# The state-space input of a fused token block read modes first and twice over, its on-chip turn dropped, and the text copy issued later

## The chip, the cores and the metric

The kernel runs on one core of a Trainium2 chip. The metric is device time in microseconds (us) of one execution. The engines that matter here are TensorE (PE), VectorE (DVE), ScalarE (ACT), GpSimd (POOL) and SyncE (SP), which issues most DMAs; each runs its own instruction stream, and semaphores join them.

## What is computed

A batch of 32 sequences is built from a diagonal state-space convolution kernel (128 rows of length 1024 for each) and 77 rows of text; one attention layer and one linear layer with low-rank parts follow. Only the first part is touched by the change:

```python
dt = exp(log_dt)                                  # (128, 2)
dt_Lambda = dt[:, None, 0] * Lambda[None, :, 0] + 1j * (dt[:, None, 1] * Lambda[None, :, 1])
Wc = (x[..., 0] + 1j * x[..., 1]) * num * _reciprocal(den * Lam, 1e-07)   # x: (32, 128, 64, 2)
K = einsum('chn,hnl->chl', Wc, exp(dt_Lambda[..., None] * pos - P_max[..., None])).real
h = concatenate([K, txt], axis=1)                 # (32, 128 + 77, 1024)
h = h + attention(layernorm(h));  h = h + linear(layernorm(h))
```

`x` holds for each of 32 sequences c, 128 rows h and 64 modes n a real and an imaginary weight.

## The kernel before

The program is a row of blocks with a barrier between them: `ssm` (the state-space part and the text copy), `prep_qkv` (weights of the projections), `attention`, `prep_out`, `output`. The order inside a block is written by hand, engine by engine, in the functions under `@block.sync`, `@block.gpsimd`, `@block.scalar`, `@block.vector` and `@block.tensor`. No scheduler moves anything: each engine takes its instructions in the order of the text and stops at its `wait_ge` lines.

`ssm` has a first part that builds tables and a loop of 16 chunks of 8 rows. In the loop (L210 to L214 on POOL, L375 to L388 on DVE, L405 to L417 on PE, L259 to L273 on ACT, L174 to L179 on SP) POOL makes the products `u` and `u2` from the weights `wr`, `wi` and the place factors `gg`; DVE makes the steps `es` from the tables `tab` and `ab` and adds `u2` to `u`; PE multiplies; ACT copies PSUM to `ob`; SP stores `ob` to the scratch tensor `hcat`. `ob` has two halves, so the copies of chunk 2 (L263, L264) wait for the stores of chunk 0.

The weights must lie with modes on the partitions, real on one half and imaginary on the other as the sums need it: `wr` and `wi` are each [128, 32 sequences, 128 rows], where partitions 64 to 127 hold the same as 0 to 63. The kernel before makes this layout on the chip. SP loads `x` into `x_sb` (the memory of `ob`) with the 128 rows h on the partitions (L168). ACT copies the real parts twice side by side into `twice[0]` (in the memory of `stage`, L231), POOL copies the imaginary parts into `twice[1]` (in the memory of `wr`, L201). PE turns them by 64 transposes against `ident` (L403), and ACT empties their PSUM tiles `pt` by 16 copies (L242, in `inputs`) into `wi` and then `wr`, eight after the second sine and eight after the fourth.

Around this lie the tables. DVE makes `f`, the two bases (L302), the small arguments, and four fractions (L323, L324) from what ACT has shifted into `turned` (L228, the memory of `es`). ACT then takes exponentials (L233, L235) and sines (L244, L246, and the four L249). POOL makes the arguments of the sizes (L197) and multiplies two of the sine tables by the sizes (L205). DVE has a long chain of small operations (L327 to L368) whose result is `gg`; it begins with a wait for the sine of L244 (L326), and its end releases the first product of POOL (L206, L213) and leads to DVE's own L373. The text copy, one DMA of 9856 KB from `txt` to `hcat`, is issued by ACT as its second instruction (L221). SP issues the load of the query weights into `stage` (L173) once the tables and the transposes are done.

Of the kernel before, what the change touches and what calls it, by code (L numbers as in the profile page):

```python
# [7 lines left out]
F32 = mybir.dt.float32  # L8
# [3 lines left out]
ALU = mybir.AluOpType  # L12
# [4 lines left out]
P = 128  # L17
B = 32
H = 128
N = 64  # L20
# [3 lines left out]
S = H + TXT  # L24
# [9 lines left out]
LA, LB, LR = 4, L // 4, 16  # L34
# [36 lines left out]
def ssm(nc, x, txt, log_dt, lam, hcat, ahead, peak):  # L71
# [4 lines left out]
    with ExitStack() as ctx:  # L76
        sb = lambda n, s, d=F32: ctx.enter_context(nc.sbuf_tensor(n, s, d))
        sem = lambda n: ctx.enter_context(nc.semaphore(n))
        wr = sb("wr", [P, B, H])
        wi = sb("wi", [P, B, H])  # L80
        ident = sb("ident1", [P, P])
        lam_sb = sb("lam_sb", [P, 2])
        ldt = sb("ldt", [P, H, 2])
        dt = sb("dt", [P, H, 2])
# [4 lines left out]
        a = sb("a", [P, H])  # L89
        b = sb("b", [P, H])  # L90
        f = sb("f", [P, H])
# [21 lines left out]
        u = sb("u", [P, 2, HC, LA, B])  # L113
        u2 = sb("u2", [P, 2, HC, LA, B])


        x_sb = ob[:].rearrange("p k j l -> p (k j l)").rearrange("p (c n t) -> p c n t", n=N, t=2)
        turned = es[:].rearrange("p k m j l -> p (k m j l)").rearrange("p (t h r) -> p t h r", t=4, r=LR)
        base = u[:].rearrange("p k j l c -> p (k j l c)").rearrange("p (h r) -> p h r", r=LR)
        base2 = u2[:].rearrange("p k j l c -> p (k j l c)").rearrange("p (h r) -> p h r", r=LR)  # L120
        bases = (base, base2)
        size = ahead[0].rearrange("p k n -> p (k n)")[:, 0:2 * H * LR].rearrange("p (k h r) -> p k h r", k=2, r=LR)
        twice = (ahead[0].rearrange("p k n -> p (k n)")[:, 2 * H * LR:].rearrange("p (c m) -> p c m", m=P), wr)
        ps = [ctx.enter_context(nc.psum_tensor(f"ps1_{i}", [P, 2, LB], F32)) for i in range(4)]
        pt = [ctx.enter_context(nc.psum_tensor(f"pt1_{i}", [P, 4, P], F32)) for i in range(2)]
        ab = [ctx.enter_context(nc.psum_tensor(f"ab1_{i}", [P, 2, HC, LR], F32)) for i in range(2)]

        in_small, in_x, txt_in = sem("in_small"), sem("in_x"), sem("txt_in")
        pool_c, dve_c = sem("pool_c"), sem("dve_c")
        dt_ok, waves_ok, la_sin_ok, la_exp_ok = sem("dt_ok"), sem("waves_ok"), sem("la_sin_ok"), sem("la_exp_ok")  # L130
        ab_ok, base_ok, turned_ok, frac_ok, sine_ok = (sem("ab_ok"), sem("base_ok"), sem("turned_ok"),
                                                       sem("frac_ok"), sem("sine_ok"))
        size_arg, size_ok, tab_cd, tab_ab = sem("size_arg"), sem("size_ok"), sem("tab_cd"), sem("tab_ab")
        args_ok, la_ok = sem("args_ok"), sem("la_ok")
        iota_ok, ident_ok = sem("iota_ok"), sem("ident_ok")
        xt_filled, xt_read = sem("xt_filled"), sem("xt_read")
        twice_ok = [sem("twice_ok0"), sem("twice_ok1")]
        gg_ok, u12_ok, ab_in, e_ok = sem("gg_ok"), sem("u12_ok"), sem("ab_in"), sem("e_ok")
        u_ok, mm_done, k_read = sem("u_ok"), sem("mm_done"), sem("k_read")
        stored = [sem("stored0"), sem("stored1")]  # L140
# [22 lines left out]
        @block.sync  # L163
        def _(sp):
            sp.dma_start(lam_sb[0:N, :], lam).then_inc(in_small, 16)
            sp.dma_start(lam_sb[N:P, :], lam).then_inc(in_small, 16)
            sp.dma_start(ldt[:], log_dt.rearrange("(o h) t -> o h t", o=1).broadcast_to([P, H, 2])).then_inc(in_small, 16)
            sp.dma_start(x_sb.rearrange("p c n t -> p c (n t)"), x.rearrange("c h n t -> h c (n t)")).then_inc(in_x, 16)  # L168

            sp.wait_ge(tab_ab, 2)  # L170
            sp.wait_ge(tab_cd, 2)
            sp.wait_ge(xt_filled, 2 * B // 4)
            sp.dma_start(ahead[0], ahead[1]).then_inc(ahead[2], 16)  # L173
            for ch in range(NCH):  # L174

                sp.wait_ge(k_read, (ch + 1) * HC // 2)
                for la in range(LA):
                    sp.dma_start(hview[la, :, ch * HC:(ch + 1) * HC, :],
                                 ob[la * B:(la + 1) * B, ch % 2, :, :]).then_inc(stored[ch % 2], 16)  # L179
            for q in range(2):  # L180
                sp.wait_ge(stored[q], 16 * LA * NCH // 2)

        @block.gpsimd
        def _(pool):
            chain = Chain(pool, pool_c)
            pool.iota(ila[:], pattern=[[LB, LA]], base=0, channel_multiplier=0,
                      allow_small_or_imprecise_dtypes=True).then_inc(iota_ok, 1)
            pool.iota(iqr[:, 0, :], pattern=[[LR, LR]], base=0, channel_multiplier=0,
                      allow_small_or_imprecise_dtypes=True).then_inc(iota_ok, 1)
            pool.iota(iqr[:, 1, :], pattern=[[1, LR]], base=0, channel_multiplier=0,  # L190
                      allow_small_or_imprecise_dtypes=True).then_inc(iota_ok, 1)
            chain(pool.memset(ident[:], 0.0))
            pool.affine_select(out=ident[:], in_=ident[:], compare_op=ALU.not_equal, fill=1.0, base=0,
                               pattern=[[-1, P]], channel_multiplier=1).then_inc(ident_ok, 1)
            pool.wait_ge(ab_ok, 1)
            for k in range(2):
                pool.tensor_tensor(size[:, k], per_row(a[:]), per_step(iqr[:, k, :]), ALU.mult).then_inc(size_arg, 1)  # L197

            pool.wait_ge(in_x, 16)
            for k in range(2):  # L200
                pool.tensor_copy(twice[1][:, :, k * N:(k + 1) * N], x_sb[:, :, :, 1]).then_inc(twice_ok[1], 1)  # L201
            pool.wait_ge(size_ok, 1)
            for t in range(2):
                pool.wait_ge(sine_ok, t + 1)
                pool.tensor_tensor(tab[:, t], tab[:, t], size[:, 0], ALU.mult).then_inc(tab_ab, 1)  # L205
            pool.wait_ge(gg_ok, 1)  # L206
            pool.wait_ge(xt_read, 2 * B // 4)

            pool.wait_ge(frac_ok, 4)
            for ch in range(NCH):  # L210
                if ch >= 2:
                    pool.wait_ge(mm_done, (ch - 1) * HC // 2)
                pool.tensor_tensor(u[:, ch % 2], by_mode(wr, ch), by_place(0, ch), ALU.mult).then_inc(u12_ok, 1)  # L213
                pool.tensor_tensor(u2[:, ch % 2], by_mode(wi, ch), by_place(1, ch), ALU.mult).then_inc(u12_ok, 1)  # L214

        @block.scalar
        def _(act):
            act.wait_ge(in_small, 48)
            act.activation(dt[:], ldt[:], ACT.Exp).then_inc(dt_ok, 1)

            act.dma_start(hcat.rearrange("(c s) d -> c s d", s=S)[:, H:S, :], txt).then_inc(txt_in, 16)  # L221

            act.wait_ge(args_ok, 1)
            act.activation(ex[:], args[:, 0].rearrange("p k h -> p (k h)"), ACT.Exp).then_inc(waves_ok, 1)
            act.activation(th[:], args[:, 0].rearrange("p k h -> p (k h)"), ACT.Tanh, scale=0.5).then_inc(waves_ok, 1)
            for t in range(4):
                act.wait_ge(base_ok, t // 2 + 1)
                act.activation(turned[:, t], bases[t // 2], ACT.Identity, bias=phase[:, t:t + 1]).then_inc(turned_ok, 1)  # L228
            act.wait_ge(in_x, 16)
            for k in range(2):  # L230
                act.copy(twice[0][:, :, k * N:(k + 1) * N], x_sb[:, :, :, 0]).then_inc(twice_ok[0], 1)  # L231
            act.wait_ge(la_ok, 1)
            act.activation(ela[:], fla[:, 0], ACT.Exp).then_inc(la_exp_ok, 1)  # L233
            act.wait_ge(size_arg, 2)
            act.activation(size, size, ACT.Exp).then_inc(size_ok, 1)  # L235

            def inputs(ns):
                for n in ns:
                    act.wait_ge(xt_filled, n + 1)
                    c = 4 * (n % (B // 4))  # L240
                    dst = (wi if n < B // 4 else wr)[:, c:c + 4, :]
                    act.copy(dst, pt[n % 2][:]).then_inc(xt_read, 1)  # L242

            act.activation(trig[:], turns[:], ACT.Sin, scale=TWO_PI).then_inc(waves_ok, 1)  # L244
            act.wait_ge(la_ok, 2)
# [1 line left out]
            for t in range(4):  # L247
                act.wait_ge(frac_ok, t + 1)
                act.activation(tab[:, t], turned[:, t], ACT.Sin, scale=TWO_PI).then_inc(sine_ok, 1)  # L249
                if t % 2:  # L250
                    inputs(range(4 * (t - 1), 4 * (t + 1)))

            def factors(ch):

# [4 lines left out]
            def results(ch):  # L259
                for j in range(HC // 2):  # L260
# [3 lines left out]
                        act.wait_ge(stored[ch % 2], 16 * LA * (ch // 2))  # L264
                    act.copy(ob[:, ch % 2, 2 * j:2 * j + 2, :], ps[n % 4][:]).then_inc(k_read, 1)

            act.wait_ge(tab_ab, 2)
            factors(0)
            factors(1)
# [123 lines left out]

        @block.tensor
        def _(pe):
            pe.wait_ge(ident_ok, 1)
            for t, n0 in ((1, 0), (0, B // 4)):
                pe.wait_ge(twice_ok[t], 2)
                for n in range(n0, n0 + B // 4):
                    if n >= 2:  # L400
                        pe.wait_ge(xt_read, n - 1)
                    for k in range(4):
                        m = pe.transpose(pt[n % 2][:, k, :], twice[t][:, 4 * (n - n0) + k, :], ident[:])  # L403
                    m.then_inc(xt_filled, 1)
            for ch in range(NCH):  # L405
                pe.wait_ge(u_ok, ch + 1)
                pe.wait_ge(e_ok, ch + 1)
                for j in range(HC):
                    n = (ch * HC + j) // 2
                    if j % 2 == 0 and n >= 4:  # L410
                        pe.wait_ge(k_read, n - 3)
                    last = 0 if j < SUMMED else 1
                    for k in range(last + 1):
                        m = pe.matmul(ps[n % 4][:, j % 2, :], u[:, ch % 2, j].rearrange("p a c -> p (a c)"),
                                      es[:, ch % 2, k, j, :], start=k == 0, stop=k == last)
                    if j % 2:
                        m.then_inc(mm_done, 1)  # L417
# [1060 lines left out]
```

## Time and profile before

| | us |
|---|---|
| three runs of the kernel before | 3353.92, 3346.96, 3353.59 (median 3353.59) |
| the profiled execution, its time | 3349.05 |
| its span from first to last instruction | 3347.3 |
| the block `ssm` in it, until the loads of the next block are issued | 212.0 |
| PE busy, share of the span | 91% |
| DVE, ACT, POOL busy | 60%, 33%, 31% |

In a row of the order of time the first number is the start in us from the start of the span, the second the length of the piece (of all `xN` instructions in it together), then engine, line, operation, output and inputs by the program's names; `[15.16 <-ACT trig L244]` says that the engine sat idle for 15.16 us before it, and what ended that. SPq and ACTq are the queues that issue DMAs; such a row is the issue, not the transfer.

### The profile page before, as it was taken

The page shows a single profiled execution, that of the slowest core. Times are in us where ns is not written, and L with a number is a line of the kernel's source. Part 1 is how long each engine was busy: PE and PEld are TensorE (multiplying, and loading weights), DVE is VectorE, ACT ScalarE, POOL GpSimd, SP SyncE. Part 2 cuts the span into 40 slices and gives each one's busy share as a digit, 9 for nine tenths or more (in the row PEclk, how much of TensorE's full clock was granted, in tenths as well). Part 3 has the DMA queues.
Part 4 walks back from the last instruction along what each step waited for, and adds up shares of the span by engine and source line. Part 5 has one row for each costly group of instructions (what it writes and reads, how often), then busy time and mean ns, then how long its engine had stood idle before and what let it go on. Part 6 is the DMA issues. An engine that isn't in the chain of part 4 may idle for free. (4 is left out here: it accounts for less than half of the span.)

```text
span 3347.3 us, 82139 instructions
## 1 busy us (share of the span) xinstructions
PE 3030.5 (91%) x29056; PEld 2239.5 (67%) x29056; DVE 2001.2 (60%) x4714; ACT 1111.7 (33%) x2452; POOL 1025.4 (31%) x1400
## 2 busy tenths in 40 slices
PE   1848799999999999999999997799999999999999
PEld 1637688888898888888888984244545454544444
DVE  7975576767676767676776765444444444443443
ACT  4331345454455455454545454210101010100100
POOL 3730344444444444444444454011101110110110
PEclk9978899999999999999999995599999999999999
DMA  4643222222222222222222213111221122122111
GB/s 147 169 126 106 47 79 56 80 53 80 56 80 55 79 68 65 70 63 78 55 78 56 71 48 136 38 67 59 75 75 64 68 75 75 56 75 75 69 62 46
DMA packets 235388, 249.64 MB, mean 75 GB/s; under 512 B 169753, under 2 KB 196505, under 8 KB 234785
## 3 DMA queue, kind: packets, MB, share of 16 engines
q1 hardware_dynamic: 234768, 234.69, 23.7%
q10 hardware_dynamic: 240, 10.09, 0.9%
q8 instruction: 214, 3.51, 0.4%
q14 instruction: 166, 1.35, 0.1%
HBM read 114.26 MB, written 80.61 MB: 58 GB/s over the span
## 5 line engine op out<-in xcount | busy, mean ns | idle before, releaser
L732 POOL TENSOR_SCALAR_AFFINE_SELECT p<-p 128x256 f32<-128x256 f32 (+1 forms) x768 | 335.3, 437 | 921.4 <-ACT p L760 899.5
L842 DVE TENSOR_REDUCE mx<-psS 77x2 f32<-77x410 f32 (+1 forms) x768 | 449.3, 613 | 242.5 <-PE psS L944 155.5
L962 PE MATMUL psJ<-xth,qh 128*128 128x205 f16 x2048 | 529.5, 259 | 10.6 <-DVE qsl L850 8.0
L964 PE MATMUL psJ<-xth,ql 128*128 128x205 f16 x2048 | 525.4, 257 | 0.0
L963 PE MATMUL psJ<-xtl,qh 128*128 128x205 f16 x2048 | 523.9, 256 | 0.0
L760 ACT ACTIVATE p<-psT,escale 128x410 f32<-128x410 f32 (+1 forms) x768 | 411.3, 572 | 282.0 <-PE psT L906 206.3
L738 POOL TENSOR_TENSOR pl<-p,ph 128x410 f16<-128x410 f32 (+1 forms) x512 | 447.1, 893 | 105.2 <-ACT ph L767 97.3
L1295 POOL TENSOR_TENSOR hb<-h,bias_sb 128x1024 f32<-128x1024 f32 x52 | 122.1, 2349 | 1045.3 <-DVE h L1337 1045.3
L929 PE MATMUL psO<-vh,pl 128*128 128x33 f16 (+2 forms) x3072 | 347.4, 187 | 0.0
L929 PE MATMUL psO<-vh,ph 128*128 128x33 f16 (+2 forms) x3072 | 341.6, 188 | 5.1 <-POOL pl L738 3.7
L929 PE MATMUL psO<-vl,ph 128*128 128x33 f16 (+2 forms) x3072 | 343.8, 187 | 0.0
L767 ACT CAST ph<-p 128x410 f16<-128x410 f32 (+1 forms) x768 | 334.1, 500 | 5.7 <-POOL p L732 5.6
L1337 DVE SCALAR_TENSOR_TENSOR h<-ps5O,osc,h_in 128x512 f32<-128x512 f32 x104 | 78.1, 751 | 429.0 <-PE ps5O L1384 429.0
L929 PEld LDWEIGHTS psO<-vh,ph 128*128 128x128 f16 (+2 forms) x3072 | 324.5, 116 | 6.8 <-issue 6.4
L929 PEld LDWEIGHTS psO<-vh,pl 128*128 128x128 f16 (+2 forms) x3072 | 325.6, 115 | 0.0
L929 PEld LDWEIGHTS psO<-vl,ph 128*128 128x128 f16 (+2 forms) x3072 | 323.9, 113 | 0.3
L1382 PE MATMUL ps5O<-woh,ath 128*128 128x512 f16 x832 | 317.1, 381 | 1.4 <-DVE atl L1322 1.4
L1383 PE MATMUL ps5O<-wol,ath 128*128 128x512 f16 x832 | 316.8, 381 | 0.0
L1382 PE MATMUL ps5F<-wfh,xth 128*128 128x512 f16 x832 | 315.3, 379 | 1.6 <-DVE xtl L1322 1.6
L1384 PE MATMUL ps5O<-woh,atl 128*128 128x512 f16 x832 | 316.6, 381 | 0.0
L1383 PE MATMUL ps5F<-wfl,xth 128*128 128x512 f16 x832 | 315.3, 379 | 0.0
L1384 PE MATMUL ps5F<-wfh,xtl 128*128 128x512 f16 x832 | 315.3, 379 | 0.0
(241 smaller groups left out, 6080.8 us busy)
## 6 DMA issues: line engine op xcount, KB each, us to landing
a_in<-acat SPq DMA_DIRECT2D x52, 512.0 KB, 4.8
h_in<-hcat SPq DMA_DIRECT2D x52, 512.0 KB, 4.2
qst<-qsh SPq DMA_DIRECT2D x512, 51.2 KB, 2.1
out<-y SPq DMA_DIRECT2D x51, 512.0 KB, 3.0
hcat<-ob SPq DMA_DIRECT2D x64, 256.0 KB, 3.7
xin<-hcat SPq DMA_DIRECT2D x32, 512.0 KB
acat<-ao SPq DMA_DIRECT2D x32, 512.0 KB
qst<-qsl SPq DMA_DIRECT2D x256, 51.2 KB, 2.1
```

The source lines that it names most:

```text
L732: pool.affine_select(out=v, in_=v, compare_op=ALU.is_ge, fill=0.0, base=0, pattern=[[0, v.shape[1]], [1, w]], channel_multiplier=-1).then_ ...
L738: pool.tensor_tensor(view(pl, g % 2, k), view(p32, g % 2, k), view(ph, g % 2, k), ALU.subtract).then_inc(lo_pool, 1)
L760: act.activation(view(p32, g % 2, k), ps_view(psT[(g + k) % 2], k), ACT.Exp, scale=(escale[:, 0:1] if k < 2 else escale[0:TXT, 0:1])).then ...
L767: act.copy(view(ph, g % 2, k), view(p32, g % 2, k)).then_inc(hi_done, 1)
L842: dve.tensor_reduce(dst, v, AX.X, ALU.max).then_inc(s_read, 1)
L929: m = pe.matmul(o[0:T[t], t, r, :], p, v[0:T[j], j, g, :], start=n == 0, stop=n == len(list_) - 1)
L962: pe.matmul(ps[:, 0:S], wh[:, k, c], xth[:, par, k, :], start=k == 0, stop=False)
L963: pe.matmul(ps[:, 0:S], wh[:, k, c], xtl[:, par, k, :], start=False, stop=False)
L964: m = pe.matmul(ps[:, 0:S], wl[:, k, c], xth[:, par, k, :], start=False, stop=k == KC - 1)
L1382: pe.matmul(ps[h][:], th[:, k, :], wh[:, k, c], start=k == 0, stop=False)
L1383: pe.matmul(ps[h][:], th[:, k, :], wl[:, k, c], start=False, stop=False)
L1384: m = pe.matmul(ps[h][:], tl[:, k, :], wh[:, k, c], start=False, stop=k == KC - 1)
```

## The change

The host hands the kernel `x` as [2, 128, 32, 128]: real or imaginary, then the 64 modes twice, then sequence and row. Two DMAs bring the two halves straight into `wr` and `wi`. What turned the input on the chip is gone: `ident`, the four copies into `twice`, the 64 transposes, the PSUM tiles `pt` and the 16 copies out of them, and the semaphores between them. The wait of POOL before its first product and of ACT before the text copy is now for both input DMAs. The text copy stands behind the fourth sine. Everything behind `ssm` is as it was.

```diff
@@ tiles and semaphores
-        ident = sb("ident1", [P, P])
-        x_sb = ob[:].rearrange("p k j l -> p (k j l)").rearrange("p (c n t) -> p c n t", n=N, t=2)
-        twice = (ahead[0].rearrange("p k n -> p (k n)")[:, 2 * H * LR:].rearrange("p (c m) -> p c m", m=P), wr)
-        pt = [ctx.enter_context(nc.psum_tensor(f"pt1_{i}", [P, 4, P], F32)) for i in range(2)]
@@ SP
-            sp.dma_start(x_sb.rearrange("p c n t -> p c (n t)"), x.rearrange("c h n t -> h c (n t)")).then_inc(in_x, 16)
+            sp.dma_start(wr[:], x[0]).then_inc(in_x, 16)
+            sp.dma_start(wi[:], x[1]).then_inc(in_x, 16)
 
             sp.wait_ge(tab_ab, 2)
             sp.wait_ge(tab_cd, 2)
-            sp.wait_ge(xt_filled, 2 * B // 4)
             sp.dma_start(ahead[0], ahead[1]).then_inc(ahead[2], 16)
@@ POOL
-            chain(pool.memset(ident[:], 0.0))
-            pool.affine_select(out=ident[:], in_=ident[:], compare_op=ALU.not_equal, fill=1.0, base=0,
-                               pattern=[[-1, P]], channel_multiplier=1).then_inc(ident_ok, 1)
-            pool.wait_ge(in_x, 16)
-            for k in range(2):
-                pool.tensor_copy(twice[1][:, :, k * N:(k + 1) * N], x_sb[:, :, :, 1]).then_inc(twice_ok[1], 1)
-            pool.wait_ge(xt_read, 2 * B // 4)
+            pool.wait_ge(in_x, 32)
@@ ACT
-            act.dma_start(hcat.rearrange("(c s) d -> c s d", s=S)[:, H:S, :], txt).then_inc(txt_in, 16)
-            act.wait_ge(in_x, 16)
-            for k in range(2):
-                act.copy(twice[0][:, :, k * N:(k + 1) * N], x_sb[:, :, :, 0]).then_inc(twice_ok[0], 1)
-            def inputs(ns):
-                for n in ns:
-                    act.wait_ge(xt_filled, n + 1)
-                    c = 4 * (n % (B // 4))
-                    dst = (wi if n < B // 4 else wr)[:, c:c + 4, :]
-                    act.copy(dst, pt[n % 2][:]).then_inc(xt_read, 1)
-                if t % 2:
-                    inputs(range(4 * (t - 1), 4 * (t + 1)))
+            act.wait_ge(in_x, 32)
+            act.dma_start(hcat.rearrange("(c s) d -> c s d", s=S)[:, H:S, :], txt).then_inc(txt_in, 16)
             act.wait_ge(tab_ab, 2)
@@ PE
-            for t, n0 in ((1, 0), (0, B // 4)):
-                pe.wait_ge(twice_ok[t], 2)
-                for n in range(n0, n0 + B // 4):
-                    if n >= 2:
-                        pe.wait_ge(xt_read, n - 1)
-                    for k in range(4):
-                        m = pe.transpose(pt[n % 2][:, k, :], twice[t][:, 4 * (n - n0) + k, :], ident[:])
-                    m.then_inc(xt_filled, 1)
@@ kernel
+        if name == "x":
+            a = np.concatenate([a.transpose(3, 2, 0, 1)] * 2, axis=1)
```

The order of ACT from its shifts to its first factors, before (the last row is the first of eight such PSUM copies; the other two sines and eight more copies follow):

```order
6 L228 ACTIVATE es<-u,phase 128x2048 [waits base_ok] x4
7 L231 COPY stage<-ob 128x32x64 [waits in_x]
8 L231 COPY stage<-ob 128x32x64
9 L233 ACTIVATE ela<-fla 128x512 [waits la_ok]
10 L235 ACTIVATE stage<-stage 128x4096 [waits size_arg]
11 L244 ACT_TABLE_LOAD
12 L244 ACTIVATE trig<-turns 128x768
13 L246 ACTIVATE tla<-wla 128x1024 [waits la_ok]
14 L249 ACTIVATE tab<-es 128x2048 [waits frac_ok] x2
15 L242 COPY wi<-pt_0 128x512 [waits xt_filled]
```

The same place of ACT in the changed kernel (its line numbers are lower: L216 is the exponential of the sizes, L223 the four sines, L240 the text copy, L229 the factors):

```order
5 L212 ACTIVATE es<-u,phase 128x2048 [waits base_ok] x4
6 L214 ACTIVATE ela<-fla 128x512 [waits la_ok]
7 L216 ACTIVATE stage<-stage 128x4096 [waits size_arg]
8 L218 ACT_TABLE_LOAD
9 L218 ACTIVATE trig<-turns 128x768
10 L220 ACTIVATE tla<-wla 128x1024 [waits la_ok]
11 L223 ACTIVATE tab<-es 128x2048 [waits frac_ok] x4
12 L240 DMA hcat<-in_txt 32x7x11264 [waits in_x]
13 L229 COPY ab_0<-tab 128x256 [waits tab_ab]
14 L229 COPY ab_1<-tab 128x256
```

No wait for the input stands ahead of the exponentials and sines any more; the first one is that of the text copy.

The order of POOL from the size arguments to the first chunk, before:

```order
12 L197 TENSOR_TENSOR stage<-a,iqr 128x2048 [waits ab_ok]
13 L197 TENSOR_TENSOR stage<-a,iqr 128x2048
14 L201 COPY wr<-ob 128x32x64 [waits in_x]
15 L201 COPY wr<-ob 128x32x64
16 L205 TENSOR_TENSOR tab<-tab,stage 128x2048 [waits sine_ok,size_ok]
17 L205 TENSOR_TENSOR tab<-tab,stage 128x2048 [waits sine_ok]
18 L213 TENSOR_TENSOR u<-wr,gg 128x1024 [waits frac_ok,xt_read,gg_ok]
```

The same place of POOL in the changed kernel:

```order
10 L186 TENSOR_TENSOR stage<-a,iqr 128x2048 [waits ab_ok]
11 L186 TENSOR_TENSOR stage<-a,iqr 128x2048
12 L191 TENSOR_TENSOR tab<-tab,stage 128x2048 [waits sine_ok,size_ok]
13 L191 TENSOR_TENSOR tab<-tab,stage 128x2048 [waits sine_ok]
14 L199 TENSOR_TENSOR u<-wr,gg 128x1024 [waits frac_ok,in_x,gg_ok]
```

The wait for the input has moved from ahead of the table products to the first product of the loop.

## Rows read from the trace of the kernel before

**Rows 1.** ACT in order of time, from the shifts to the first factors
```profile
20.21 7.67 ACT L228 ACTIVATE es<-u,phase 128x2048 f32<-128x2048 f32 x4
44.64 3.97 ACT L231 COPY stage<-ob 128x2048 f32<-128x2048 f32 x2 [16.77 <-DMA ob<-in_x]
48.52 0.63 ACT L233 ACTIVATE ela<-fla 128x512 f32<-128x512 f32 x1
...
55.66 3.69 ACT L249 ACTIVATE tab<-es 128x2048 f32<-128x2048 f32 x2
...
59.26 1.05 ACT L242 COPY wi<-pt 128x512 f32<-128x512 f32 x2
...
75.75 0.69 ACT L257 COPY ab<-tab 128x256 f32<-128x256 f32 x2
```

**Rows 2.** DVE in order of time, from its last fraction to the loop
```profile
37.39 2.29 DVE L324 TENSOR_TENSOR es<-es,tab 128x2048 f32<-128x2048 f32 x1
54.84 0.42 DVE L327 SCALAR_TENSOR_TENSOR t<-ex,th 128x256 f32<-128x256 f32 x1 [15.16 <-ACT trig L244]
...
57.41 0.35 DVE L336 SCALAR_TENSOR_TENSOR cc<-em,lam_sb,cc 128x128 f32<-128x128 f32 x1
57.68 4.69 DVE L337 SCALAR_TENSOR_TENSOR cc<-em,lam_sb,cc 128x128 f32<-128x128 f32 x1
62.40 4.51 DVE L338 TENSOR_TENSOR cc<-cc 128x128 f32<-128x128 f32 x1
66.83 0.28 DVE L339 TENSOR_TENSOR cc<-cc 128x128 f32<-128x128 f32 x1
...
77.44 0.42 DVE L368 TENSOR_SCALAR gg<-fla 64x512 f32<-64x512 f32 x1
77.89 6.83 DVE L373 TENSOR_TENSOR tab<-tab,stage 128x2048 f32<-128x2048 f32 x2
...
103.43 4.48 DVE L382 TENSOR_TENSOR es<-tab,ab 128x2048 f32<-128x2048 f32 x2 [3.56 <-ACT ab L257]
```

**Rows 3.** POOL in order of time, first part of the block
```profile
44.67 4.00 POOL L201 COPY wr<-ob 128x2048 f32<-128x2048 f32 x2 [30.58 <-DMA ob<-in_x]
57.70 9.06 POOL L205 TENSOR_TENSOR tab<-tab,stage 128x2048 f32<-128x2048 f32 x2 [9.03 <-ACT tab L249]
77.94 4.63 POOL L213 TENSOR_TENSOR u<-wr,gg 128x1024 f32<-128x1024 f32 x1 [11.18 <-DVE gg L368]
```

**Rows 4.** PE and ACT in order of time, at the loop's start
```profile
93.67 14.87 PE L414 MATMUL ps<-es,u 128*128 128x256 f32 x56 [18.43 <-DVE u L388]
...
111.00 0.59 ACT L265 COPY ob<-ps 128x512 f32<-128x512 f32 x1 [1.56 <-PE ps L414]
...
116.18 0.59 ACT L265 COPY ob<-ps 128x512 f32<-128x512 f32 x1 [1.14 <-PE ps L414]
```

**Rows 5.** Stretches: length, busy (instructions) by engine, PE clock, DMA share, GB/s
```profile
60.00:62.00 2.00, 2.00 (x10) 1.78 (x11) 2.00 (x1) 1.01 (x3) 2.00 (x1) 1.00 0.00 0
70.00:72.00 2.00, 2.00 (x10) 1.77 (x11) 1.92 (x5) 1.02 (x3) 0.00 (x0) 0.50 0.00 0
86.00:98.00 12.00, 4.33 (x10) 3.53 (x11) 11.96 (x6) 0.58 (x1) 6.53 (x3) 0.50 0.86 346
99.00:100.00 1.00, 1.00 (x7) 0.87 (x6) 0.87 (x1) 0.59 (x1) 0.00 (x0) 1.00 0.00 0
130.00:160.00 30.00, 27.91 (x124) 23.33 (x125) 27.23 (x17) 11.77 (x23) 23.76 (x10) 1.00 0.61 150
```

**Rows 6.** DMA queue of the text copy and DMA issues, 0 to 110 us
```profile
q10 hardware_dynamic: 240, 10.09, 27.2%
...
hcat<-in_txt ACTq DMA_DIRECT2D x1, 9856.0 KB, 39.5
stage<-in_L_attn_wq SPq DMA_DIRECT2D x1, 4096.0 KB, 12.7
...
ob<-in_x SPq DMA_DIRECT2D x1, 0.5 KB, 41.7
```

More of the change, by code:

```diff
@@ L122, in ssm @@
         size = ahead[0].rearrange("p k n -> p (k n)")[:, 0:2 * H * LR].rearrange("p (k h r) -> p k h r", k=2, r=LR)
-        twice = (ahead[0].rearrange("p k n -> p (k n)")[:, 2 * H * LR:].rearrange("p (c m) -> p c m", m=P), wr)
         ps = [ctx.enter_context(nc.psum_tensor(f"ps1_{i}", [P, 2, LB], F32)) for i in range(4)]
-        pt = [ctx.enter_context(nc.psum_tensor(f"pt1_{i}", [P, 4, P], F32)) for i in range(2)]
         ab = [ctx.enter_context(nc.psum_tensor(f"ab1_{i}", [P, 2, HC, LR], F32)) for i in range(2)]
         in_small, in_x, txt_in = sem("in_small"), sem("in_x"), sem("txt_in")
-        pool_c, dve_c = sem("pool_c"), sem("dve_c")
+        dve_c = sem("dve_c")
         dt_ok, waves_ok, la_sin_ok, la_exp_ok = sem("dt_ok"), sem("waves_ok"), sem("la_sin_ok"), sem("la_exp_ok")
@@ L134, in ssm @@
         args_ok, la_ok = sem("args_ok"), sem("la_ok")
-        iota_ok, ident_ok = sem("iota_ok"), sem("ident_ok")
-        xt_filled, xt_read = sem("xt_filled"), sem("xt_read")
-        twice_ok = [sem("twice_ok0"), sem("twice_ok1")]
+        iota_ok = sem("iota_ok")
         gg_ok, u12_ok, ab_in, e_ok = sem("gg_ok"), sem("u12_ok"), sem("ab_in"), sem("e_ok")
@@ L184, in _ @@
         def _(pool):
-            chain = Chain(pool, pool_c)
             pool.iota(ila[:], pattern=[[LB, LA]], base=0, channel_multiplier=0,
@@ L395, in _ @@
         def _(pe):
-            pe.wait_ge(ident_ok, 1)
-            for t, n0 in ((1, 0), (0, B // 4)):
-                pe.wait_ge(twice_ok[t], 2)
-                for n in range(n0, n0 + B // 4):
-                    if n >= 2:
-                        pe.wait_ge(xt_read, n - 1)
-                    for k in range(4):
-                        m = pe.transpose(pt[n % 2][:, k, :], twice[t][:, 4 * (n - n0) + k, :], ident[:])
-                    m.then_inc(xt_filled, 1)
             for ch in range(NCH):
@@ L1464 @@
     for name in _INS:
-        a = np.ascontiguousarray(inputs[name])
+        a = np.asarray(inputs[name])
+        if name == "x":
+            a = np.concatenate([a.transpose(3, 2, 0, 1)] * 2, axis=1)
+        a = np.ascontiguousarray(a)
         if a.dtype == np.bool_:
```

## The prediction

> **What bounds the kernel now.** I read the order of time of ACT first, since the change takes a wait out of it; then DVE, which ACT releases; POOL, which both feed; then the stretches and the DMAs. The input lands late: 41.7 us after its issue, beside a text copy that takes 39.5 us [rows 6]. ACT has finished its shifts at 20.21 + 7.67 = 27.88, sits idle for 16.77 us until the input is there, and copies it before it goes on to the exponential of L233 at 48.52 [rows 1]. So ACT does everything from L233 on 48.52 - 27.88 = 20.64 us later than its own work would let it. POOL has nothing to do in that time (30.58 us idle) [rows 3]. What reaches the end is smaller, and stands in DVE: it finishes its fourth fraction at 37.39 + 2.29 = 39.68 and waits 15.16 us for the sine of L244 [rows 2]. From 54.84 on, it runs without a gap to `gg` at 77.86, releases POOL's first product at 77.94 [rows 2, 3], and PE starts the loop at 93.67 [rows 4]. In the loop DVE is busy for 27.23 of 30 us [rows 5], so it sets the pace, and the block's end moves by what its start moves. The 15.16 us are therefore about what can be had; ACT's 20.64 are not, because DVE's own fractions end only at 39.68.
>
> **The change, part by part.**
>
> *The wait and the copies on ACT go (L231).* ACT starts L233 at 27.88 (its argument was ready before, at DVE's pace). From L233 to the first sine L249 it took 55.66 - 48.52 = 7.14 us [rows 1], the table load among it; so the first sine starts at 35.02. Trig is then ready well before DVE asks for it at 39.68. The first three sines ask for their fractions at 35.0, 36.9 and 38.7; DVE begins the second step of the fourth at 37.39 [rows 2], so the third is there in time, and the two before it, each two DVE operations earlier, as well.
>
> *A new meeting of POOL and DVE.* POOL's two products L205 take 9.06 us together and began 2.04 us after the first sine started [rows 1, 3]; now they begin at 37.1, in DVE's last fraction. While POOL ran them before, two tiny DVE operations took 4.69 and 4.51 us, where their neighbours of the same shape took 0.35 and 0.28 [rows 2]. So one of the two engines stands while the other works: 4.34 + 4.23 = 8.57 us of DVE's chain were such standing. DVE's chain from L327 to `gg` without it is 77.86 - 54.84 - 8.57 = 14.45 us. Whatever the order in which they take turns, DVE has its fraction and its chain to do and stands for POOL's whole 9.06 us: `gg` comes at 39.68 + 14.45 + 9.06 = 63.19 instead of 77.86. That is 14.67 us earlier. In other words: the idle 15.16, less 9.06 - 8.57 = 0.49 of more standing. The bounds: if DVE didn't have to stand at all, `gg` would come at 54.13, a gain of 23.7; I take the sum with standing, since two rows show it with exactly this POOL instruction. The other side is that DVE stands twice, once for the last fraction and then again for a later pair, but there is no later POOL instruction before `gg`.
>
> The Trainium skill, "SBUF — State Buffer", section "Who interferes with whom", says the same of VectorE operations with two inputs in SBUF beside a GpSimd one that reads it: whoever is first holds the shared ports for a whole instruction. Without it the sum would be the 23.7; the trace agrees with it by the two rows above.
>
> *The fourth sine* waits for a fraction that POOL's first product may push to 39.68 + 4.53 = 44.2; it ends at about 46.1 and is wanted by DVE's L373 at 63.2. Hidden by 17 us.
>
> *The transposes and PSUM copies go.* 64 transposes on PE, 16 copies of about 0.53 to 0.59 us on ACT between the sines [rows 1]: they ended at about 75.9, ahead of `gg` at 77.86, so they weren't what POOL waited for. Nothing is gained by itself. But at 63.2 they would be late, so the gain needs their removal. The factors (L257 at 75.75 before) wait for POOL's second product, now at about 48.7 to 49, and are wanted only at about 63.2 + 6.8 = 70: hidden. The identity and POOL's two copies are early or in idle time: nothing.
>
> *The input as two DMAs of 2 MB.* It is first wanted by POOL at 63.2, and at about 46 by ACT ahead of the text copy. The trace doesn't show this load. The nearest row is the load of query weights, as large (4096 KB) and alone on the queues: 12.7 us [rows 6]; the farthest is the present input, 2 MB in 41.7 us beside the text. Issued at about 3, both halves land at about 16 by the first and at 3 + 2 x 41.7 = 86 by the second. I take the first: nothing runs beside them now. In that case 47 us of slack are left.
>
> *The text copy moves behind the fourth sine* and is issued at about 47. Its issue costs ACT 0.7 us, hidden since ACT then waits for POOL until 48.7. Its packets were 27.2% of 110 us on the DMA engines, that is 29.9 us of their time [rows 6]; at most it takes the 39.5 us of the row. So it ends between 78 and 87. SP issues the query weights when L373 is done, at 84.7 - 14.7 = 70, so these two now overlap, and behind the weights on the same queue stand the stores of chunk 0, issued from 103.1 - 14.7 = 88.5. The weights had 0.86 of 12 us [rows 5], 10.3 us of DMA time. Text done by 78 or so: text and weights end at 70 + 1.5 + 6.5 + 10.3 = 88, just ahead of the stores, and nobody waits. At the bound of 39.5: about 98; the stores of chunk 0 are 1 MB, and the loop's 150 GB/s at a DMA share of 0.61 over 30 us [rows 5] make 18.3 / 4.5 = 4.1 us a MB, so they land at 102, and ACT's first copy of chunk 2, before at 111.00, now at 96.3, would stand 5.7 us. It can catch up (116.18 - 111.00) - 3 x 0.59 = 3.4 us, because it is paced by PE at 1.73 us a copy and needs 0.59 [rows 4]. So between 0 and 2.3 us; I take 0, since 29.9 is the packets' own time and 39.5 has the old input in it.
>
> *PE's clock.* The matmuls of chunk 0 run at a granted clock of 0.50, the lower level of 1.2 GHz, until about 99, when the clock rises to the full 2.4 GHz [rows 5]. They started at 93.67 after 18.43 us of idleness [rows 4]. In the changed kernel PE does nothing before 79, so I take the same slow start: no change. The clock column says 1.00 at 60 to 62, after a far longer pause; but ten transposes take the same 2 us there as at 70 to 72 with 0.50 [rows 5], so the column cannot be believed before its first change.
>
> The Trainium skill, "TensorE: Matmul & The Clock Gate", section "What's actually happening", has the throttled clock as the state from which activity releases the engine; the trace agrees by the equal pace of the transposes. If the column were right the start would be fast instead, which is the second rival.
>
> *The sum:* -15.16 + 0.49 = -14.7 us. On the profiled execution: 3349.05 - 14.7 = 3334.4. The median of the three runs lies 4.5 us above that execution; on it: 3353.59 - 14.7 = 3338.9, which is my time.
>
> **The rivals.**
>
> 1. DVE doesn't stand for POOL in the new place, because its last fraction and the early part of its chain slip past. For it: only L337 and L338 are seen standing. Against: both inputs of nearly every operation of the chain are of the same sort. Gain up to 23.7: 3329.9.
>
> 2. The clock is full in chunk 0. Then PE doesn't hold DVE at chunk 2, where DVE was idle for 3.56 us [rows 2]; chunk 0's matmuls would take about 6.3 us instead of 8.9, gain 2.6 more: 3336.3. Against: the equal pace of the transposes.
>
> 3. Text copy, query weights and stores pile up as worked out above: 2.3 us given back, 3341.2.
>
> 4. The change does what it says in `ssm`, and the rest of the program takes it back. Everything behind the block's barrier starts earlier by the same amount, with the same instructions, so I see no mechanism; but the runs alone are spread over 7 us. Within 0.2%: about 3350.
>
> 5. Slower than before: the new loads are slow. If 4 MB come at the rate of the old input, they land at 86, POOL's first product moves from 77.94 to 86, and the time is 3353.59 + 8.1 = 3361.7. It decides at a landing of 77.9: earlier is a gain, later a loss. Against it: the old input had the text copy beside it and rows of 512 bytes, and the new rows are 16 KB each.
>
> **How the numbers follow.** The forecast 0.64, rival 1 0.06, rival 2 0.08, rival 3 0.08, rival 4 0.09, rival 5 0.05. A measurement of this kernel can tell about 0.2% (6.7 us) from no change. Faster by more than that: the first four, 0.86; within it 0.09; slower 0.05. The range reaches down to the lowest run less the gain with rival 2 (3346.96 - 17.3 = 3329.7), a little beyond it for rival 1, and up to the edge of "no change" (3346.9): 3328 to 3347.
>
> **What would show it.** ACT's exponential of L233 (now L214) at about 27.9; the wait of DVE for trig gone; two DVE operations of some 4.5 us or a stretched fraction between 37 and 49; `gg` at 63.2; the first matmul at 79.0 at the lower clock; the input landed by 20; the text copy landed between 78 and 87; the loads of the next block issued at 197.3 instead of 212.0. It would be wrong if the input landed after 63, if DVE's chain took another length than 14.5 plus 9.1, or if ACT stood at the first copy of chunk 2.

## The result, and the profile after

The changed kernel takes 3369.5 us (median, 3336.9 to 3379.0), the kernel before 3349.5 us beside it (3345.6 to 3365.4). The ratio of the means is 1.0044, with a 95% interval of 1.0024 to 1.0063: slower by 0.44%, where 0.44% faster was forecast (the medians alone make 1.0060: four of the twenty executions of the changed kernel took under 3355 us, the others 3362 to 3379). The profiled execution took 3362.45 us with a span of 3360.6, 13.3 more than before.

In `ssm` it went as forecast. ACT, DVE, POOL and SP in order of time, after (start, length, engine, line, then the idle time before it; they answer to [rows 1 to 4]):

```profile
29.35 0.61 ACT L214 ACTIVATE ela<-fla 128x512 f32<-128x512 f32 x1
...
45.47 1.91 ACT L223 ACTIVATE tab<-es 128x2048 f32<-128x2048 f32 x1 [3.50 <-DVE es L298]
45.48 0.72 ACTq L240 DMA_DIRECT2D hcat<-in_txt  x1
...
97.18 0.58 ACT L237 COPY ob<-ps 128x512 f32<-128x512 f32 x1 [1.56 <-PE ps L379]
```

```profile
6.91 0.15 DVE L260 TENSOR_SCALAR g<-lam_sb 128x1 f32<-128x1 f32 x1 [5.30 <-DMA ldt<-in_L_tok_log_dt]
...
38.95 6.48 DVE L298 TENSOR_TENSOR es<-es,tab 128x2048 f32<-128x2048 f32 x1
45.36 4.72 DVE L301 SCALAR_TENSOR_TENSOR t<-ex,th 128x256 f32<-128x256 f32 x1
...
63.69 0.42 DVE L342 TENSOR_SCALAR gg<-fla 64x512 f32<-64x512 f32 x1
```

```profile
38.52 11.28 POOL L191 TENSOR_TENSOR tab<-tab,stage 128x2048 f32<-128x2048 f32 x2 [22.86 <-ACT tab L223]
64.20 4.63 POOL L199 TENSOR_TENSOR u<-wr,gg 128x1024 f32<-128x1024 f32 x1 [14.40 <-DVE gg L342]
```

```profile
79.93 14.80 PE L379 MATMUL ps<-es,u 128*128 128x256 f32 x56 [79.93 <-DVE u L362]
...
198.19 0.41 SPq L414 DMA_DIRECT2D st_k<-in_L_attn_wk  x1
```

The last row is the first load of the next block, which the kernel before issued at 211.99: 13.8 us won. The DMA issues of the first 110 us (KB, then us to landing), after:

```profile
hcat<-in_txt ACTq DMA_DIRECT2D x1, 9856.0 KB, 36.3
stage<-in_L_attn_wq SPq DMA_DIRECT2D x1, 4096.0 KB, 21.5
...
wr<-in_x SPq DMA_DIRECT2D x1, 2048.0 KB, 9.4
wi<-in_x SPq DMA_DIRECT2D x1, 2048.0 KB, 13.8
ldt<-in_L_tok_log_dt SPq DMA_DIRECT2D x1, 128.0 KB, 4.7
```

The loss lies behind it. `output` starts its first product later, before (L1382) and after (L1347):

```profile
2164.91 0.61 PE L1382 MATMUL ps5O<-woh,ath 128*128 128x512 f16 x1 [1.40 <-DVE atl L1322]
```

```profile
2178.26 0.61 PE L1347 MATMUL ps5O<-woh,ath 128*128 128x512 f16 x1 [1.40 <-DVE atl L1287]
```

That is 13.35 us late, the whole difference of the spans, so `output` itself is unchanged. What lies between, whose code the change does not touch, takes 27.2 us more: 13.8 won at its start, 13.35 lost at its end. Nearly all of it is in `attention`, whose first product comes 13.8 us earlier than before (244.27 and 258.07) and whose last ends 13.8 us later (2077.1 and 2063.3). `attention` is mostly a hardware loop of 13 turns of two steps; the jump back to its start is called the wrap here. A turn took 109.66 us before and 111.39 after (the mean of the 11 turns between the 12 wraps), which makes 19.0 of the 27.2 us; the rest is lost in the steps before the first wrap and behind the last. The views of waits over 460 to 2140 us (us in total, times, longest) say who waits longer; before, then after:

```profile
ACT vsh L775 <- DMA vl<-vsl: 81.5, 16, 6.2
...
PE psT L906 <- ACT p L760: 13.0, 19, 1.5
```

```profile
ACT vsh L740 <- DMA vl<-vsl: 88.9, 14, 7.1
...
PE psT L868 <- issue: 38.7, 12, 3.5
...
PE psT L871 <- ACT p L725: 26.5, 23, 2.4
```

TensorE's wait for ACT's exponential `p` doubles; its wait for "issue" (for nothing that the view names) at L868 is 37.8 us before (L903) and 38.7 after, 12 times some 3 us, at the wrap. One turn shows the chain, before and after (SP's row, ACT, PE in order of time):

```profile
1187.43 2.96 SPq L635 DMA_DIRECT2D kst<-ksh  x4
...
1204.35 0.37 ACT L775 CAST vsh<-psJ 128x256 f16<-128x256 f32 x1 [4.52 <-DMA vl<-vsl]
```

```profile
1179.79 2.43 SPq L600 DMA_DIRECT2D kst<-ksh  x4
1182.27 3.33 SPq L600 DMA_DIRECT2D kst<-ksl  x4
...
1188.17 5.77 SPq L600 DMA_DIRECT2D qst<-qsh  x8
1193.99 2.68 SPq L600 DMA_DIRECT2D qst<-qsl  x4
...
1198.75 0.59 SPq L628 DMA_DIRECT2D vl<-vsl  x1
```

```profile
1203.61 0.37 ACT L740 CAST vsh<-psJ 128x256 f16<-128x256 f32 x1 [6.41 <-DMA vl<-vsl]
...
1204.54 0.48 PE L871 MATMUL psT<-qst,kst 98*77 98x308 f16 x1 [1.73 <-ACT p L725]
```

SP issues a row of 24 small copies (`restack`), some 0.6 us each, then the copy of `vl`. ACT may not write `vsh` before these copies have read it; behind that wait stands the exponential, and TensorE waits for this. Four issues take 2.43 us, but 3.33 in the second group of this row (before, the one group with a fetch takes 2.96). In that group's time one packet was fetched on the queue q8 (DMA queues, 1182.2 to 1185.6, and the whole execution before and after). q8 brings TensorE's own program; it is read so because each of TensorE's waits at the wrap has such a packet at its start (see e8):

```profile
q8 instruction: 1, 0.02, 2.4%
```

```profile
q8 instruction: 214, 3.51, 0.5%
```

```profile
q8 instruction: 225, 3.69, 0.5%
```

3.51 MB in 214 packets is 16.4 KB a packet; by the period of 256 instructions that e9 and e10 find, that is 64 bytes an instruction. Of the issues of L635 between 470 and 1840 us that took over 0.9 us, 87 of 91 had such a fetch beginning within 0.5 us of their start, of the shorter ones 53 of 1111; after, 90 of 91 and 84 of 1086. So a long issue nearly always has a fetch beside it, but many a fetch has no long issue. The critical row, the one ahead of the second step of a turn, meets one fetch in 10 of 12 turns before (from its first issue to its last it takes 15.3 us on average) and two in every turn after (16.2 us). The whole execution has 11 fetches more than before, about one a turn. After the wait the clock falls, and TensorE goes at the lower of its two levels, 1.2 GHz, for some 3 us (length, busy by engine, granted clock in the third number from the end; the first stretch lies ahead of the wait, the second behind it):

```profile
1199.00:1200.00 1.00, 1.00 (x11) 0.90 (x10) 0.82 (x6) 0.00 (x0) 0.00 (x0) 1.00 0.88 327
1204.60:1207.20 2.60, 2.60 (x16) 2.30 (x17) 1.67 (x3) 2.10 (x5) 1.82 (x4) 0.50 0.08 30
```

So the suspicion was: the change made TensorE's compiled program 130 instructions shorter (64 transposes are 64 weight loads and 64 matmuls, and 2 waits), which moves `attention` by half a block of 256 against the borders at which the program is fetched. "Place" below means where TensorE's program stands against these borders.

### The profile page after: what moved, and what is told of

Read it like the earlier page. It is cut to its first block and busy times, and to the rows that moved or that the text cites. A ratio compares the mean times of both kernels' runs of the same rounds, so it can differ in the third digit from the quotient of the medians.

```text
span 3360.6 us, 81794 instructions
## 1 busy us (share of the span) xinstructions
PE 3013.5 (90%) x28800; PEld 2235.7 (67%) x28992; DVE 2001.5 (60%) x4714; ACT 1098.8 (33%) x2434; POOL 1021.9 (30%) x1396
## 5 line engine op out<-in xcount | busy, mean ns | idle before, releaser
L1347 PE MATMUL ps5O<-woh,ath 128*128 128x512 f16 x832 | 317.1, 381 | 1.4 <-DVE atl L1287 1.4
L1347 PE MATMUL ps5F<-wfh,xth 128*128 128x512 f16 x832 | 315.3, 379 | 1.6 <-DVE xtl L1287 1.6
```

Of the source, the lines that this page charges most:

```text
L1347: pe.matmul(ps[h][:], th[:, k, :], wh[:, k, c], start=k == 0, stop=False)
```

## Experiments

The ratios are to runs of the kernel before on the same chip (medians 3354.8 us beside e1 to e4, 3348.2 beside e5 to e8, 3349.2 beside e9 to e12). All kernels but e5 and e12 compute everything. "Fillers" are instructions that do nothing, put ahead of TensorE's first wait in `ssm`, where it has nothing to do until about 80 us:

```diff
+        fill = sem("fill")
@@ ssm, first lines of @block.tensor
+            for _ in range(130):
+                pe.sem_inc(fill, 1)
```

T1 is the theory of the place of TensorE's program; the rivals are named in the expectations. Where an expectation puts TensorE's wait in front of the row scores, it follows my first reading; the view of waits puts it one instruction earlier, at `psT` for ACT.

**e1, changed kernel with 130 fillers (the old place).** 

> The changed kernel with 130 semaphore increments as fillers at the start of TensorE's part of the state-space block, where TensorE is idle for 79 us. They take the place of the 130 instructions (64 weight loads, 64 matmuls, 2 waits) that the change took out of TensorE's program, so that everything behind stands where it stood before in that program. Theory T1 (the place of TensorE's program against its 16 KB fetches decides when a fetch meets SyncE's row of small DMA issues in the attention loop, and that costs the loop its 27 us): the block keeps its gain of 13.8 us, the attention loop runs as in the kernel before, and the time is about 14 us below the kernel before: 3335, ratio 0.996. Rival T2 (the loop is slower because it starts 14 us earlier, or because the larger input has moved the tensors in memory): no help, the time stays about 3369, ratio 1.005.

Measured: 3341.6 us (3335.3 to 3346.0), ratio 0.9958 [0.9943, 0.9974]. One fetch in the row in 11 of 12 turns, 15.3 us, a turn 109.98 us. TensorE's wait for ACT:

```profile
PE psT L874 <- ACT p L728: 17.6, 21, 2.1
```

**e2, kernel before with 126 fillers (the place of the changed one).** 

> The kernel before with 126 semaphore increments at the start of TensorE's part of the state-space block: 126 + 130 = 256 instructions of 64 bytes are one fetch of 16 KB, so TensorE's program stands against the fetches as in the changed kernel, with nothing else changed. T1: the attention loop becomes 20 to 27 us slower, 3369 to 3377, ratio about 1.007, with the same wait of TensorE at the row scores of the loop's second half. T2: unchanged within 0.2%, ratio 1.000.

Measured: 3377.0 us (3375.1 to 3388.7), ratio 1.0073 [1.0054, 1.0092]. Two fetches in the row, 16.2 us, a turn 111.96.

```profile
PE psT L909 <- ACT p L763: 26.6, 22, 3.0
```

The loss is larger than the time shows: in the profiled execution the input landed in 37.5 us instead of 41.7, and `ssm` was done at 207.38 instead of 211.99, so what lies between `ssm` and `output` takes 31.6 us more than before.

These two are the crossed test: the loss goes with the place of TensorE's program, not with the new input or the earlier start. e1 has all of the change and is faster than before; e2 has none of it and is slower. The other engines' programs, also a little shorter, weren't put back in e1 and aren't needed for it: the packets on q14, the other queue of kind "instruction", fell from 177 before to 118 after, and are 118 in e1 too and 179 in e2.

**e3 and e4, 64 and 194 fillers.** 

> The changed kernel with 64 fillers: half way between the changed kernel's place and the old one. T1: a time of its own between 3330 and 3375; the wait of TensorE at the row scores in the loop's second half follows how many of its fetches fall into SyncE's issues ahead of it. I expect about 3350. T2: 3369, as with any number of fillers.

> The changed kernel with 194 fillers, 64 beyond the old place. T1: a time of its own between 3330 and 3375, not equal to that with 130 fillers; I expect about 3345. T2: 3369, as with any number of fillers.

Measured: e3 3363.9 us, 1.0025 [1.0000, 1.0049]; e4 3346.5 us, 0.9974 [0.9963, 0.9985]. e3 was expected near 3350 and came out 14 us higher; e4 met its 3345. Both have two fetches in every row (16.3 and 16.2 us), but in e4 TensorE waits little for ACT:

```profile
PE psT L874 <- ACT p L728: 11.4, 15, 2.2
PE psT L871 <- DMA qst<-ml: 10.4, 15, 1.0
```

So the number of fetches in one row doesn't settle it: e4 waits less than e3 for ACT with as many, and more for another copy of SP. Nor does the number of all fetches: both have 226.

**e5, no fillers, the row of 24 issues cut to 20.** It leaves out part of the computation: the low halves of the second half of the stacked queries stay zero (the lines shown are the cut itself; the waits for these copies count 8 instead of 12, and a memset puts the zeros). 

> The changed kernel without fillers, where SyncE's row of issues at the start of each attention step is 20 DMAs long instead of 24: the third part of the second half of the heads' stacked queries (the low halves) isn't copied, and holds zeros instead (the part of the computation that is left out); the waits count 8 DMAs there instead of 12. TensorE's program is longer by 2 instructions only, so its fetches fall as in the changed kernel. T1 (the late arrival of that row is what TensorE waits for at the row scores): the row takes about 13.5 us instead of 16.2, the wait of 1.85 us an iteration goes, an iteration takes about 109 us instead of 111.7, and the time falls by 25 us or more, to 3345 or below. Rival T3 (the fetches slow TensorE itself, and SyncE only stands by): the iterations stay at 111 to 112 us, the time at 3365 to 3370.

```diff
-                    restack(Q_PARTS, qst[nxt], HALVES[1], q_in[1])
+                    restack(Q_PARTS[0:2], qst[nxt], HALVES[1], q_in[1])
```

Measured: 3325.1 us (3323.7 to 3328.8), 0.9936 [0.9913, 0.9959]. The first row here is `vl`, the second TensorE:

```profile
ACT vsh L741 <- DMA vl<-vsl: 42.8, 11, 5.1
...
PE psT L872 <- ACT p L726: 3.7, 10, 0.4
```

The row still meets two fetches, but takes 13.6 us, some 2.6 less, and TensorE's wait for ACT is gone, in the bad place of TensorE's program: the row's length is what this wait comes from. It is worth 44 us against the changed kernel, more than the place cost, so the row isn't free in the good place either; the short row was not tried there.

**e6, 130 fillers, and the two input loads wait until the small loads have landed.** 

> The changed kernel with 130 fillers, and the two input DMAs issued only when the three small loads have landed. In the changed kernel the last small load landed 1.5 us later than before, beside the input. Theory: the small load lands at 5.3 again, every step up to the factors gg is 1.5 us earlier than with 130 fillers alone, the input still lands by 25, and the time is 1.5 us lower (3340), which the times alone can hardly show. Rival (the small load is late for another reason): it lands at 6.8 again, no change.

```diff
+            sp.wait_ge(in_small, 48)
             sp.dma_start(wr[:], x[0]).then_inc(in_x, 16)
```

Measured: 3338.3 us (3331.4 to 3344.6), 0.9971 [0.9957, 0.9984]. `ldt` lands in 3.1 us instead of 4.5 in e1, and the last operation on `gg` starts at 62.06 instead of 63.50:

```profile
ldt<-in_L_tok_log_dt SPq DMA_DIRECT2D x1, 128.0 KB, 3.1
```

The next block's loads are issued at 196.87, not 197.85. So that was the missing microsecond in `ssm`; the whole time is too coarse to show it.

**e7, 130 fillers, text copy again early on ACT.** 

> The changed kernel with 130 fillers, and the text copy issued where the kernel before issued it, as ScalarE's second instruction, so that it runs beside the input. Theory: the input lands later (between 25 and 50 us instead of 17) but is wanted by GpSimd only at 63, so the factors and the first matmul stay where they are within 1 us, and the query weights land in 12.7 us again instead of 21.5: time equal to that with 130 fillers within 3 us. Rival (the later text copy is what makes room for the input): the input lands behind 63 and the state-space block gives back what it gained, up to 14 us.

Measured: 3341.7 us, 0.9984 [0.9965, 1.0004], in `ssm` as e1 (`gg` at 63.67, next loads 197.96). The DMA issues:

```profile
hcat<-in_txt ACTq DMA_DIRECT2D x1, 9856.0 KB, 39.2
...
wr<-in_x SPq DMA_DIRECT2D x1, 2048.0 KB, 12.9
wi<-in_x SPq DMA_DIRECT2D x1, 2048.0 KB, 36.2
```

Beside the text the second half lands at about 39, still over 20 us before it is wanted. Moving the text copy bought nothing in `ssm`, and nothing that the whole time can tell.

**e8 and e9, 98 and 98 + 256 = 354 fillers.** 

> The changed kernel with 98 fillers: TensorE's fetches in the loop come 32 instructions, about a microsecond, later than with 130. T1: the first place between 130 (one fetch in the row, 3341.6) and 64 (two, 3364); the time follows the number of fetches in the row, 3338 to 3345 with one, 3355 to 3365 with two. T2: no rule.

Measured: 3403.2 us (3385.5 to 3407.6), 1.0152 [1.0122, 1.0181], a turn 115.31 us. My forecast was some 40 us too low. The row meets three fetches in 11 of 12 turns (16.1 us), but the larger part is new. The waits, then the start of a turn in order of time:

```profile
PE psT L871 <- issue: 68.9, 24, 3.5
...
PE psT L874 <- ACT p L728: 27.9, 23, 3.0
```

```profile
1256.69 0.52 PE L871 MATMUL psT<-qst,kst 98*128 98x410 f16 x1 [2.86 <-issue]
1259.93 0.50 PE L871 MATMUL psT<-qst,kst 98*128 98x410 f16 x1 [2.72 <-issue]
```

"issue" is a wait for nothing that the view names. Every kernel here has one of some 3 us at the wrap (12 times); this one has a second behind the first matmul (24 times). The packets of q8 say what they are. In each of the 14 traces every wait of this kind (over 2 us, in the loop) has a packet of q8 that begins within 0.9 us of the wait's start, and TensorE goes on 2.2 to 3.4 us after it began (12 of 12 waits; 24 of 24 in e8, e9 and e12; in e11 there are two packets, and TensorE goes on 3.1 to 4.2 us after the second). In the turn shown, packets begin at 1254.09 and 1257.14. So TensorE waits for its program at the wrap, and in this place once more for the block behind.

> The changed kernel with 354 = 98 + 256 fillers. Theory T1 (what counts is where TensorE's program lies against its 16 KB fetches, so only the number of instructions modulo 256 counts): as with 98 fillers, ratio 1.015 to the kernel before (1.010 to 1.020), an iteration of attention's loop near 115 us, TensorE waiting some 3 us at the loop's first scores. Rival T4 (the 98-filler result is a matter of the number of instructions, of this one build or of chance): ratio between 0.995 and 1.005, iteration 110 to 112 us.

Measured: 3393.8 us (3385.6 to 3400.7), 1.0144 [1.0101, 1.0187], a turn 114.35.

```profile
PE psT L871 <- issue: 70.1, 24, 3.6
```

**e10, 130 + 256 = 386 fillers.** 

> The changed kernel with 386 = 130 + 256 fillers. T1: as with 130, ratio 0.996 (0.993 to 0.998), one fetch of TensorE in SyncE's row of 24 issues, iteration 110.0 us. T4: another number, for instance near 1.004 like the changed kernel itself; if the fillers cost time by their number, 256 of them show in the start of the first matmul of the state-space loop (79 us), though TensorE has nothing to do before it.

Measured: 3334.3 us (3330.6 to 3341.6), 0.9961 [0.9946, 0.9977], a turn 109.05, one fetch in every row. The first matmul of `ssm` starts at 80.19 (79.74 in e1), so the fillers themselves hold nothing up. e9 and e10 show the period: adding 256 instructions changes nothing beyond the intervals, adding 32 (98 to 130) changes the time by 1.9%. T4 falls.

**e11, 162 fillers.** 

> The changed kernel with 162 fillers, between 130 (0.996) and 194 (0.997). T1 with a place that changes step by step: ratio 0.996 to 0.998, iteration 110 to 110.8 us. T4 (no order in the places): anything between 0.993 and 1.015, as 98 against 130 would suggest.

Measured: 3358.3 us (3354.4 to 3369.8), 1.0028 [1.0008, 1.0048]: T1 with a smooth change falls, and with it the count of fetches in the row as the measure: it is one in 10 of 12 turns (15.4 us). ACT is nearly in time, but SP's copy of `ml` is late and the wrap takes longer, with two packets of q8 in each of its 12 waits instead of one:

```profile
PE psT L871 <- issue: 47.9, 12, 4.4
...
PE psT L871 <- DMA qst<-ml: 11.5, 15, 1.1
...
PE psT L874 <- ACT p L728: 6.8, 16, 1.2
```

**e12, e5's short row with e8's place** (it leaves out what e5 does). 

> SyncE's row of 20 issues instead of 24 (the low halves of the second half of the stacked queries stay zero and are not copied) together with the place of 98 fillers, which with 24 issues gave 1.015. T1 with its price in the row alone: the row ends 2.5 us earlier, TensorE no longer waits in the second step, and the time is that of 20 issues without fillers, 3325 us, within 6. T1 with a second place (TensorE's wait at the loop's first scores is behind another row, which is not shortened): that part stays, some 3 us in each of 13 iterations, 3355 to 3368 us. T5 (the fetches hold TensorE itself, whatever SyncE does): the whole loss of 98 fillers against 130 stays, 62 us, so 3380 us or more.

Measured: 3357.1 us (two of ten executions 3337.1, the others 3354.2 to 3360.1), 1.0019 [0.9995, 1.0043].

```profile
PE psT L872 <- issue: 69.6, 24, 3.7
...
PE psT L875 <- ACT p L729: 3.5, 10, 0.4
```

It lies 32 us above e5 and 46 below e8: the row's part went, the second wait at the wrap stayed. The two are separate costs of one place.

The kernels that compute everything and differ in TensorE's place alone, by place (fillers, less 256 where there are more; the kernel before stands at 130). The waits are TensorE's at `psT` over 460 to 2140 us, for issue, ACT and `ml` together:

| place | kernel | median us | ratio | fetches on q8 | waits us |
|---|---|---|---|---|---|
| 0 | changed | 3369.5 | 1.0044 | 225 | 66.9 |
| 0 | e2 (before) | 3377.0 | 1.0073 | 226 | 66.0 |
| 64 | e3 | 3363.9 | 1.0025 | 226 | 61.3 |
| 98 | e8 | 3403.2 | 1.0152 | 226 | 97.5 |
| 98 | e9 | 3393.8 | 1.0144 | 227 | 95.5 |
| 130 | before | 3349.5 | 1 | 214 | 51.5 |
| 130 | e1 | 3341.6 | 0.9958 | 214 | 56.6 |
| 130 | e10 | 3334.3 | 0.9961 | 215 | 50.2 |
| 162 | e11 | 3358.3 | 1.0028 | 226 | 66.2 |
| 194 | e4 | 3346.5 | 0.9974 | 226 | 60.5 |

The place of the kernel before is the only one tried that is fetched with one packet less a turn, and the best; that it is the best was luck, and e4 comes within 0.2% of it with the packet more. The waits put the changed kernels nearly in the order of their times; e3 and e11 stand the wrong way round. The time grows more than the waits: by 64.5 us against 40.9 from e1 to e8 in the profiled executions (3341.75 and 3406.24). The clock can make up the rest, though its share was not measured apart. In `attention` it was granted at the lower level for 155.5 us in e1 and 240.6 in e8, and TensorE's products L930 to L932 start every 0.17 us at that level and every 0.09 at the other, so 85 us more of it cost up to 40 us. That is an estimate from above, since TensorE also stands idle in that time. Before and after it is 160.0 and 187.6 us.

## Why the prediction was wrong

**The step that failed** is one sentence: "Everything behind the block's barrier starts earlier by the same amount, with the same instructions, so I see no mechanism." The instructions are the same, but not their place in TensorE's program, and the change took 130 away ahead of a loop that lives off SP's row being just in time. It cost 27.2 us between `ssm` and `output` (profile after), against the 14.7 hoped for. The loss has two parts that the runs show: SP's row of issues is longer by 0.9 us where it meets two fetches (e5 takes this wait away), and in other places TensorE's own wait for its program grows (e8, e11). The mechanism had to be looked for in three views that I left out: the waits of the loop, which name `vl` and the wrap's issue gap in the kernel before already; the q8 line of the page; and the count of instructions that an edit removes. Rival 4 was right in kind and too small, and stopped at "same"; the one rival on the slow side was put in `ssm`.

**`ssm`, point by point.** Forecast a gain of 14.7, measured 13.8.

- The 15.16 us that the sum starts from are one execution's. In e2's, the kernel before with fillers, the input landed in 37.5 us instead of 41.7, DVE waited 10.21 us for trig, and the block was done 4.6 us earlier.
- ACT's exponential at 27.9: it came at 29.35. The term missed was the small load `ldt`: 4.7 us instead of 3.2 with 4 MB behind it on the same queue. e6 gives it back. "Nothing runs beside them now" was said of the big loads; the small one beside them wasn't costed.
- DVE's wait for trig is gone. The two engines met as forecast: L298 took 6.48 instead of 2.29, L301 4.72 instead of some 0.42, 8.5 us of standing against 9.06 in the sum, and POOL's pair took 11.28 instead of 9.06. `gg` was done at 64.1, forecast 63.2; without `ldt`'s delay it comes at 62.5 (e6). Rival 1 falls.
- Input landed at 12.1 and 17.0 (forecast: by 20). Rival 5 falls, and by e7 it would even beside the text.
- Text copy landed at 45.5 + 36.3 = 81.8, inside 78 to 87. The query weights took 21.5 us beside it and landed at 92.6, not 88; still ACT's copy of chunk 2 stood for PE and not for a store (97.18). Rival 3 falls.
- First matmul at 79.93 (79.0) with the 56 matmuls in 14.80 us, as [rows 4] had 14.87: no full clock from the start, rival 2 falls.

**In sum:** with TensorE's program put back in its place, e1, e6 and e10 are 13.2, 9.9 and 14.8 us below the kernel before beside them, where 14.7 was forecast; e7, with the text copy early, is 6.5 below, and its interval reaches 1. The sum for `ssm` was sound; its reach wasn't.

**What stays open.** Why a fetch that falls into an issue makes it longer is not shown; only that they coincide. That the second wait in e8 is for a block that begins right behind the jump's target is argued from the fetch at its start and from the period; no trace names the instructions in a packet. Nor is it shown by how much the longer row alone accounts for the changed kernel's loss: the short row in the good place is missing. The changed kernel's own executions run from 3336.9 to 3379.0, wider than before; why some of them escape is open, since the one profiled is not among them. And 130 fillers are no remedy: any edit ahead of the loop moves the place again. What lasts is slack in SP's row, as e5 shows by leaving some of it out.

## What to carry to other kernels

An edit that removes instructions moves everything behind it in that engine's program, and a hardware loop further on may then be fetched at other moments. A kernel may sit in a good place by luck, as this one did, and then an edit that saves work can still lose time. Before a gain of under 1% is forecast or believed, try the kernel with fillers of a few sizes in an idle place of the engine that sets the pace, and look in the loop for waits that are just covered. When a result goes the other way, cross it: the new code in the old place, and the old code in the new place.

## What the runs showed of the hardware

- The same kernel, with 98, 130, 162 or 194 idle instructions of TensorE in front, takes 3403, 3342, 3358 or 3347 us, and 256 more of them change nothing beyond the intervals (354: 3394; 386: 3334).
- The Trainium skill, "Runtime: NRT & Kernel Launch", section "Instruction fetch mechanics", has engines fetch their program in blocks of 16 KiB, 256 instructions, over a DMA queue of their own, and has a taken branch whose target lies outside the window of two blocks wait until the block is fetched. The trace agrees with 16.4 KB a packet, the period of 256 in e9 and e10, and the wait of some 3 us at each wrap with a packet of q8 beginning at its start. The section also calls the cost of crossing a block "mostly hidden"; here the measurement decides otherwise: 32 instructions of shift make 1.9% of the whole.
- The cost of a fetch showed on another engine: an issue of SP takes up to 2.1 us (the longest of L635 in the loop) instead of 0.59, and 87 of 91 that take over 0.9 have a fetch of TensorE's beginning within 0.5 us, against 53 of 1111 of the others.
- A load of 128 KB that is issued 0.6 us before two large ones lands in 4.5 to 5.0 us (eleven traces); alone it lands in 3.1 (e6).
